# A deformable-convolution kernel on one core: moving entries in the table that places one image's preparation beside another's convolution

## The reference

```
x = x + attention(group_norm(x))       # q k^T over channels, softmax, v, output projection
x = x + deform_conv(group_norm(x))     # then batch norm over all images, gelu
```

## Time and profile before

| | |
|---|---|
| median of three runs | 4038.47 us |
| profiled execution | 4037.25 us, of which span 4035.5 us |
| TensorE busy | 3538.2 us, 88% |
| VectorE busy | 2500.6 us, 62% |
| ScalarE busy | 2101.5 us, 52% |
| GpSimd busy | 1416.7 us, 35% |
| mean granted TensorE clock | 0.945 of full speed |

### The profile page before, as it was taken

The page is one execution under the profiler, slowest core; times in us unless marked ns, Lnnn a source line. Parts: engine busy times, 40 slices in busy tenths (PEclk is TensorE's granted clock), DMA queues, the critical chain, the costliest instruction groups (busy, mean ns, idle before and its releaser), DMA issues.

```text
span 4035.5 us, 107978 instructions
## 1 busy us (share of the span) xinstructions
PE 3538.2 (88%) x38307; PEld 3088.6 (77%) x38307; DVE 2500.6 (62%) x5517; ACT 2101.5 (52%) x4790; POOL 1416.7 (35%) x1225
## 2 busy tenths in 40 slices
PE   3899999999999999999999999999999999999700
PEld 1788888888888888888888888888888888888600
DVE  3566666666666666666666666666666666666522
ACT  1455555555555455555555555555555555555432
POOL 1333333433433333333333333333334333333311
PEclk8999999999999999999999999999999999999855
DMA  2001111101011111001111111011111010111399
GB/s 77 22 27 45 45 37 45 45 28 43 28 45 37 45 45 45 28 31 40 45 37 45 45 40 33 27 45 45 37 45 45 28 42 30 45 37 34 84 370 312
DMA packets 101918, 225.01 MB, mean 56 GB/s; under 512 B 36289, under 2 KB 62081, under 8 KB 101377
## 3 DMA queue, kind: packets, MB, share of 16 engines
q1 hardware_dynamic: 90784, 191.76, 15.0%
q0 software_dynamic: 7168, 25.17, 1.6%
q10 hardware_dynamic: 3424, 0.90, 0.1%
HBM read 87.29 MB, written 75.50 MB: 40 GB/s over the span
## 4 chain that ended last, share of the span: by engine, by line
PE 61%; issue 14%; DMA 9%; POOL 6%; DVE 4%; ACT 3%; SPq 2%; POOLq 0%; DVEq 0%; ACTq 0%
PE sps L729 10%; PE acc L746 7%; PE acc L747 7%; PE acc L748 7%; DMA x2s<-x 4%; POOL sT L1363 4%; PE zps L715 3%; PE zps L716 3%; PE zps L717 3%; PE zps L718 3%; PE zps L719 3%; DMA xn<-x_scratch 2%; PE l L591 2%; DMA out<-x 1%; PE l L590 1%
## 5 line engine op out<-in xcount | busy, mean ns | idle before, releaser
L1363 POOL TENSOR_TENSOR sT<-ay,bx 128x768 f32<-128x768 f32 x768 | 1140.0, 1492 | 1387.7 <-PE sps L729 1302.2
L1174 DVE TENSOR_TENSOR sl<-sps,sh 128x384 f16<-128x384 f32 x1536 | 848.7, 553 | 629.9 <-ACT sh L942 618.5
L746 PE MATMUL acc<-zh,sh 128*128 128x192 f16 x4608 | 1147.6, 249 | 18.0 <-ACT ypm L963 18.0
L747 PE MATMUL acc<-zl,sh 128*128 128x192 f16 x4608 | 1146.3, 249 | 0.5 <-issue 0.5
L748 PE MATMUL acc<-zh,sl 128*128 128x192 f16 x4608 | 1145.6, 249 | 0.0
L942 ACT CAST sh<-sps 128x384 f16<-128x384 f32 x1536 | 736.6, 480 | 679.4 <-PE sps L729 669.5
L918 ACT CAST zh<-zps 128x288 f16<-128x288 f32 x1536 | 617.1, 402 | 728.6 <-PE zps L719 710.6
L1168 DVE TENSOR_TENSOR zl<-zps,zh 128x288 f16<-128x288 f32 x1536 | 695.9, 453 | 428.2 <-ACT zh L918 425.8
L729 PE MATMUL sps<-eye,sT 128*128 128x128 f32 x4608 | 790.2, 281 | 152.5 <-POOL sT L1363 126.1
L729 PEld LDWEIGHTS sps<-eye,sT 128*128 128x128 f32 x4608 | 554.4, 143 | 256.0 <-issue 156.2
L746 PEld LDWEIGHTS acc<-zh,sh 128*128 128x128 f16 x4608 | 456.9, 99 | 28.1 <-ACT ypm L963 23.0
(11 more groups left out here) (176 smaller groups left out, 5369.3 us busy)
## 6 DMA issues: line engine op xcount, KB each, us to landing
x2s<-x SPq DMA_DIRECT2D x64, 767.2 KB, 5.2
xin<-in_x SPq DMA_DIRECT2D x32, 512.0 KB, 5.2
xin<-in_x SPq DMA_DIRECT2D x64, 256.0 KB, 5.7
x_scratch<-x SPq DMA_DIRECT2D x32, 512.0 KB, 3.0
y_scratch<-ych SPq DMA_DIRECT2D x32, 512.0 KB, 3.3
zh<-y_scratch SPq DMA_DIRECT2D x20, 512.0 KB, 10.8
zl<-x_scratch SPq DMA_DIRECT2D x20, 512.0 KB, 12.1
out<-zh POOLq DMA_DIRECT2D x20, 512.0 KB, 8.9
```

What stands on the lines that cost most here:

```text
L746: pe.matmul(acc[:, 0:C], s_h, zh[:, j, ky, z], start=start and kx == 0, stop=False)
L747: pe.matmul(acc[:, 0:C], s_h, zl[:, j, ky, z], start=False, stop=False)
L1174: dve.tensor_tensor(one(sl), sps[u % 2][:, 0:3 * P], one(sh), ALU.subtract).then_inc(s_lo, 1)
L1363: pool.tensor_tensor(sT[:, p % ST_RING].rearrange("p k (r x) -> p k r x", r=R), a, x_, ALU.mult)\
```

## The change

Entries of PLAN move, and some are split. In the first group norm, moments0 goes from unit -5 to -6, rstd0 from -2 to 0, norm0 to norm3 from units -1 to 2 into 0 to 3, low2 and low3 a unit later. In the second, norm7, low5, low6 and low7 go a unit later. The mask, the row activations and the column hats get entries of their own: mask0 stays in 41, row_act0 stands in 42, row_hats0 in 43; columns0 in 42 and columns1 in 43; column_hats0 in 43 and column_hats1 in 46. So part 1 of the column hats is made before the image starts, instead of after product 1 and in unit 4. The last transposes of y of the image before go from unit 1 to 0, their scaling from unit 5 to 1. The shift is issued plane by plane as each plane is ready, eight DMAs in place of four, the wrapped rows last.

```
-  ... -5: ("moments0",), -3: ("group0",), -2: ("rstd0",), -1: ("norm0",), 0: ("norm1",),
-  1: ("norm2", "low0"), 2: ("norm3", "low1"), 3: ("low2",), 4: ("low3",), 6: ("turn_x0",), ...
+  ... -6: ("moments0",), -3: ("group0",), 0: ("rstd0", "norm0"), 1: ("norm1",),
+  2: ("norm2", "low0"), 3: ("norm3", "low1"), 4: ("low2",), 5: ("low3",), 6: ("turn_x0",), ...
-  28: ("norm6", "low4"), 29: ("norm7", "low5"), 30: ("low6",), 31: ("low7",),
+  28: ("norm6", "low4"), 29: ("low5",), 30: ("norm7",), 31: ("low6",), 32: ("low7",),
-  36: ("edges0",), 38: ("offsets0",), 39: ("offsets1",), 40: ("clip0",), 41: ("rows0",),
-  42: ("columns0", "row_hats0"), 44: ("rows1",), 45: ("row_act1",), 46: ("row_hats1",)}
+  36: ("edges0",), 38: ("offsets0",), 39: ("offsets1",), 40: ("clip0",), 41: ("rows0", "mask0"),
+  42: ("row_act0", "columns0"), 43: ("columns1", "column_hats0", "row_hats0"),
+  44: ("rows1",), 45: ("row_act1",), 46: ("row_hats1", "column_hats1")}
-  TURN_LAST_Y, SCALE_LAST_Y = 1, 5
+  TURN_LAST_Y, SCALE_LAST_Y = 0, 1
```

```
 def shift(b, par):                                        # SyncE
-    sp.wait_ge(xn_lo, 8 * b + 8)
-    ... x2w first rows, x2w last rows, all planes left, all planes right: four DMAs
+    for k in range(3):
+        if k == 0:
+            sp.wait_ge(xn_hi, 4 * b + 3)
+        else:
+            sp.wait_ge(xn_lo, 8 * b + 4 + 2 * k)
+        sp.dma_start(side(0)[:, 1:N], plane[:, k, 0:N - 1]).then_inc(x2_shifted, 16)
+        sp.dma_start(side(1)[:, 0:N - 1], plane[:, k, 1:N]).then_inc(x2_shifted, 16)
+    sp.dma_start(seam(0), plane[:, :, N - WRAP * W:N]).then_inc(x2_shifted, 16)
+    sp.dma_start(seam(1), plane[:, :, 0:WRAP * W]).then_inc(x2_shifted, 16)
-  if u in (4, 14, 24):                                    # ScalarE, part 1
-      column_hats((4, 14, 24).index(u) + 1, b, par)
+  if u in (14, 24):
+      column_hats((14, 24).index(u) + 2, b, par)
-  pool.wait_ge(x2_shifted, 64 * b + 64)                   # GpSimd, edges
+  pool.wait_ge(x2_shifted, 128 * b + 128)
-  if p in (1, 4, 10):                                     # GpSimd, part 1
-      column_distance((1, 4, 10).index(p) + 1, b, par)
+  if p in (4, 10):
+      column_distance((4, 10).index(p) + 2, b, par)
```

More of the change, by code:

```diff
@@ L331, in all_pairs @@
                 step(ROUNDS, i)
-        PLAN = {-10: ("x_stats0", "x_stats1"), -9: ("x_stats2", "x_stats3"), -5: ("moments0",), -3: ("group0",),
[2 rows of a table removed]
+        PLAN = {-10: ("x_stats0", "x_stats1"), -9: ("x_stats2", "x_stats3"), -6: ("moments0",), -3: ("group0",),
[2 rows of a table added]
                 10: ("gram0",), 11: ("gram_wq0",), 12: ("logits0",), 13: ("exp0",), 14: ("prob0",),
@@ L476, in shift @@
             def shift(b, par):
-                sp.wait_ge(xn_lo, 8 * b + 8)
+                seam = lambda h: x2w_all[:, :, par, h * WRAP * W:(h + 1) * WRAP * W]
                 plane = x2_all[:, :, par, PAD_T * W:PAD_T * W + N]
[L480 to L485, removed]
+                for k in range(3):
[3 more added lines that the diff above has]
+                        sp.wait_ge(xn_lo, 8 * b + 4 + 2 * k)
+                    side = lambda h: x2s_all[:, k, h, PAD_T * W:PAD_T * W + N]
+                    sp.dma_start(side(0)[:, 1:N], plane[:, k, 0:N - 1]).then_inc(x2_shifted, 16)
+                    sp.dma_start(side(1)[:, 0:N - 1], plane[:, k, 1:N]).then_inc(x2_shifted, 16)
+                sp.dma_start(seam(0), plane[:, :, N - WRAP * W:N]).then_inc(x2_shifted, 16)
+                sp.dma_start(seam(1), plane[:, :, 0:WRAP * W]).then_inc(x2_shifted, 16)
             def convolved(b):
@@ L892, in part0 @@
                     normalize(q % 2, i, x1, inner(x2[2 * i], par), 1, b)
-                if stage == "rows0":
+                if name == "mask":
                     act.wait_ge(off_sb, b + 1)
                     act.activation(mask[:, par], off[:, par, :, 2 * TAPS:J], ACT.Tanh, scale=0.5)
-                if stage in ("rows0", "row_act1"):
+                if name == "row_act":
                     h = q
@@ L902, in part0 @@
                     act.activation(d, d, ACT.Relu, scale=-1.0, bias=1.0).then_inc(hat_act, 1)
-                if name == "columns":
-                    column_hats(0, b, par)
+                if name == "column_hats":
+                    column_hats(q, b, par)
             def column_hats(q, b, par):
@@ L1331, in part0 @@
                 if name == "columns":
-                    column_distance(0, b, par)
+                    column_distance(q, b, par)
             def edges(b):
-                pool.wait_ge(x2_shifted, 64 * b + 64)
+                pool.wait_ge(x2_shifted, 128 * b + 128)
                 pool.sem_inc(edges_due, 1)
```

## The result

The changed kernel takes 3852.17 us (median of four runs, 3848.88 to 3854.67) against 4038.47 before: a ratio of 0.954, 95% interval 0.951 to 0.957. The forecast was 3862. A fourth run of the kernel before took 6985.66 us and is left out of its median, as its other runs, here and beside every experiment, lie between 4026 and 4048. The span of the profiled execution goes from 4035.5 to 3847.1 us, so 188.4 us are to be found in it.

The account below looks back on a forecast made before the run. TensorE was taken as the bound, its stalls mostly behind GpSimd's sT. 4037.25 - 126 (stall) - 55 (clock) - 19 (sl) - 14 (x2s) + 15 + 24 (added waits) = 3862 us; range 3820 to 3935.

Parts of the forecast that it names:

- Stall behind sT, -126: At unit 46 TensorE waits for GpSimd's sT, held behind rstd of another image; the whole stall goes, some 126 us.
- Clock, -55: Behind the stall TensorE runs at half clock; without the gap 1.8 us are saved 30 times, 55 us.
- sl, -19: TensorE's 0.61 us wait in unit 44 goes, as ScalarE's wait leaves unit 41: about 19 us, bounds 0 and 23.
- x2s, -14: Shift by plane opens the zeroed edges about 2 us sooner, so TensorE's 14.3 us behind x2s go.
- my lower bound of 3.6: A 256 KB side of the shift was to land 3.6 to 5.7 us after its issue.
- Added waits, +15 and +24: column_hats1 in unit 46 delays convolve(0) by 0.5 us, 15 in all; low3 in unit 5 delays turn_x0 by 0.8, 24.
- The rivals: the first: The sT stall at unit 46 only shrinks, 2 us remain: 3922, or 3976 with the slow clock; chance 0.13.
- its doubt about the chain: Chains from ScalarE to DVE to ScalarE to GpSimd in neighbouring units might make the first sT late, against 1.5 us slack.
- The second: The shift's eight DMAs come through one behind another, edges open 8.5 us later: slower, 4195; chance 0.04.
- its mild form: Each shift DMA pays a fixed cost of about 2 us in turn, edges open 2 us later: an estimated 3944.
- The third: GpSimd stands behind another wait (columns1 or hats) at the same place, as long as today: 4037; chance 0.04.

Follow-up runs that it names:

- moments_back: The changed kernel with moments0 alone put back to unit -5: 3937.84 us, ratio 0.975.
- hats_back: The changed kernel with the entries of mask, row activations, columns and hats put back as before the change: 4036.49 us, ratio 0.999.
- rstd_alone: The kernel before with only rstd0, norm0 to norm3, low2 and low3 moved as in the change: 4074.56 us, ratio 1.0092.
- rstd_m7: The kernel before with rstd0, norm0 to norm3, low2 and low3 moved as in the change, and moments0 at -7: 3977.26 us, ratio 0.985.

## Why the prediction was right, and what it did not see

- **Stall behind sT, -126:** measured -125.7. The order on GpSimd and the first product's time came as laid (1659.6, laid at 1861.4 - 202.0 = 1659.4, with 202.0 between the two traces' columns0). TensorE asked 0.6 us sooner than I had it.
- **Clock, -55:** no slow stretch is left between images. In the trace before, the two units behind the stall last 58 us longer in 30 changes than two units of 1.68. What the other terms leave of 188.4 (below) is some 54 us, a remainder that holds their errors too.
- **sl, -19:** the label gives 23.4 to 4.3, -19; the stretch from unit 44's transposes to the end of the group sums is 0.38 us shorter beyond that, 12 in 31 changes. So -31, the largest miss: the label counts only the idle time ahead of one unit, and the next unit starts late too, without a label.
- **x2s, -14:** -14, and 3.3 (16.4 to 13.1 us) before the first image, where I had nothing. A side of 256 KB lands in 2.4 us, below my lower bound of 3.6, which came from transfers to and from HBM.
- **Added waits, +15 and +24:** +16.7 and +25.0. Reading ypm from norm6's row and turn_x0 from low3's end and the product's hold gave both labels to 2 us.
- **Sum:** -125.7 - 31 - 14.3 - 3.3 + 16.7 + 25.0 = -132.6; 188.4 - 132.6 = 55.8 are left, of which 1.4 is a shorter wait for the first constants (22.2 to 20.8 us); the rest is put down to the clock.

So the forecast held with its terms, for the change as a whole, and most of the 10 us that it lacks are those of sl. As an account of the parts it was incomplete, and in part lucky. The new order of units 42 and 43 was laid with moments0 at 0.8 us, a guess about length that came out right only because the change puts moments0 ahead of the hats. I gave its move no price; moments_back measures it at 86 us, and hats_back the hats' entries at 184, where the sum had 19 less 15. The earlier scaling of the last y, put at nothing, keeps up to 27 us from turn_x0. I had used the hold of a low beside a product (1.38 against 0.69) for turn_x0 and not asked where else the freed products would run beside VectorE. The stall that the change removes had kept GpSimd idle for 8.56 us, and moments0 ran in that time.

The rivals: the first fell (no sT wait left), though its doubt about the chain was the right place to look, as the slack was 0.7 us. The second fell (the DMAs overlap, edges 4.1 us behind the last plane), and its mild form with it; the section of the Trainium skill that this form rests on, DMA: Bandwidth & Descriptors, Anatomy of one DMA, gives its figure for DMAs issued by GpSimd, and the shift goes by SyncE's queue. The third fell for the whole change, but it is what rstd_alone and hats_back do: the wait is replaced and the time stays.

Not tried: a kernel in which moments0 itself reads PSUM or one input only, and what that would save; that the hold goes by the operation's form is seen on other operations only.

## What to carry to other kernels

A wait that goes on one engine starts that engine's work earlier, and what ran beside its idle time now runs beside its work: list the short operations of the other engines in that stretch before pricing the gain. Here two multiplies of 0.16 us, a unit or two too late, took back 86 to 123 us. Parts of a schedule change are not additive: rstd0 with its norm and low stages alone gave +36 us, everything but rstd0 gave -4, next to nothing, and the whole gave -186.

## What the runs showed of the hardware

- A VectorE operation of 128x2 with both inputs in SBUF took 0.16 us beside an idle GpSimd and 1.04 to 1.42 in the rows above, where it started inside a GpSimd product or column distance (rstd_alone, hats_back, moments_back, and gvar in the changed kernel, which ends at 1664.18 against 1664.17). Over all kept traces 548 of these small operations started inside an operation of GpSimd: 488 of them ended 0.01 to 0.02 us behind it, and the other 60 started within 0.05 us of its end. None that started outside took over 0.2 us. Operations with one input in SBUF took the same time inside and outside (sl, 0.56 us). The Trainium skill states this in SBUF — State Buffer, section Who interferes with whom: a VectorE instruction with two SBUF inputs contends with a GpSimd instruction that reads SBUF, as its second input comes through a read interface that they share, and this contention is an exclusive lock. The rows agree to the end time; what they add is the price of the place, 86 us for one unit.
- The clock fell to half behind a wait of 1.56 us of the group sums in moments_back, in 22 changes of image of 30, and behind a wait of 2.25 us at turn_x0 in 27 of 30 in rstd_alone but 9 of 30 in rstd_m7 (counted by the units behind the wait, which together last about 1 us or more longer where it fell). Within one trace the same wait at the same place had both outcomes, as the two windows of rstd_m7 above show. So neither the length of a gap nor the work right around it decides alone; what does is not shown. Window of moments_back behind one of its waits:

```profile
1705.50:1708.50 3.00, 3.00 (x20) 2.62 (x18) 2.42 (x10) 2.43 (x6) 2.16 (x4) 0.53 0.00 0
```
